# Cross attention on one core: P times values in runs of one to three tiles, maximum products chunk by chunk, and other slots for keys, values and the turning

## The reference

```
x = x + attention(layernorm(x))                 # token and channel diffusion
x = x + cross(layernorm(x), ctx_1024)           # the stage that the change touches
x = x + experts(layernorm(x))                   # top 2 of 8 experts

cross(query, value):                            # 16 heads, depth 8
    q, k, v = query @ wq.T + bq, value @ wk.T + bk, value @ wv.T + bv
    attn = softmax(q k^T / sqrt(8))             # per head, 56 x 1500
    return (attn v) @ wo.T + bo
```

## Time and profile before

| | |
|---|---|
| median of 3 runs | 646.7 us (645.82 to 649.69) |
| profiled execution | 653.12 us |
| its span, first to last instruction | 651.3 us |
| mean granted clock of TensorE | 0.96 |
| busy, share of the span | TensorE 91%, VectorE 66%, ScalarE 52%, GpSimd 28% |

### The profile page before, as it was taken

One profiled execution on the slowest core, in us unless ns is written; L12 is line 12 of the kernel. 1 busy time (PEld: TensorE's weight loads), 2 busy tenths in 40 slices (PEclk: granted clock), 3 DMA queues, 4 the chain that ended last, 5 costly groups with the idle time before them and its releaser, 6 DMA issues. The chain is left out here.

```text
span 651.3 us, 17561 instructions
## 1 busy us (share of the span) xinstructions
PE 593.1 (91%) x6732; PEld 481.7 (74%) x6732; DVE 427.2 (66%) x799; ACT 338.2 (52%) x506; POOL 183.2 (28%) x149
## 2 busy tenths in 40 slices
PE   3799787798999999999999999999985699999997
PEld 1566374376877877877877787787774589999997
DVE  4765357866887788778788788877822464444443
ACT  2466445274666576567566566657564353333321
POOL 4685305622223323224223232322100221111100
PEclk9789789798999999999999999999998599999999
DMA  5000006498267356446536736734620011111100
GB/s 211 1 3 3 0 3 133 94 193 192 68 132 183 96 140 144 119 117 142 144 92 141 172 88 127 179 100 91 144 100 1 17 46 49 48 48 48 48 17 29
DMA packets 26190, 60.29 MB, mean 93 GB/s; under 512 B 14368, under 2 KB 15392, under 8 KB 26152
## 3 DMA queue, kind: packets, MB, share of 16 engines
q1 hardware_dynamic: 26152, 59.77, 38.3%
HBM read 20.48 MB, written 0.46 MB: 32 GB/s over the span
## 5 line engine op out<-in xcount | busy, mean ns | idle before, releaser
L1163 DVE TENSOR_REDUCE chunk_max<-PS 128x1 f32<-128x500 f32 x336 | 214.3, 673 | 62.2 <-PE PS L1283 60.5
L1103 ACT ACTIVATE P<-PS 125x896 f32<-125x896 f32 x192 | 173.3, 913 | 124.1 <-PE PS L1307 123.4
L1283 PE MATMUL PS<-k_hi,q_block_hi 128*128 128x500 f32 x336 | 131.3, 438 | 6.5 <-ACT k_full L246 3.3
L1307 PE MATMUL PS<-q_stack,k_stack 97*125 97x224 f32 x768 | 122.5, 283 | 4.3 <-DMA q_stack<-neg_rows 2.4
L1307 PEld LDWEIGHTS PS<-q_stack,k_stack 97*125 97x125 f32 x768 | 106.9, 190 | 19.3 <-issue 8.9
L255 POOL TENSOR_TENSOR k_lo<-k_full,k_hi 128x500 fp32r<-128x500 f32 x48 | 61.1, 1276 | 104.7 <-ACT k_full L246 102.4
L1283 PEld LDWEIGHTS PS<-k_hi,q_block_hi 128*128 128x128 f32 x336 | 60.9, 193 | 37.1 <-ACT k_full L246 16.7
L1629 DVE TENSOR_TENSOR hidden<-gated,PS 128x448 f32<-128x448 f32 x64 | 39.6, 619 | 69.2 <-PE PS L1686 63.8
L1323 PE MATMUL PS<-P,values 125*32 125x112 f32 x3072 | 84.4, 262 | 0.6 <-ACT P L1103 0.5
L1323 PEld LDWEIGHTS PS<-P,values 125*32 125x32 f32 x3072 | 72.6, 110 | 14.3 <-issue 10.8
L1541 ACT ACTIVATE gated<-PS 128x448 f32<-128x448 f32 x64 | 34.8, 544 | 80.5 <-PE PS L1686 76.0
(11 more groups left out here) (153 smaller groups left out, 666.7 us busy)
## 6 DMA issues: line engine op xcount, KB each, us to landing
k_stack<-k_hi SPq DMA_DIRECT2D x128, 187.5 KB, 4.5
ctxT<-ctx_in SPq DMA_DIRECT2D x16, 750.0 KB, 4.3
k_stack<-k_lo SPq DMA_DIRECT2D x64, 187.5 KB, 4.4
w_gate_up<-wgu_in SPq DMA_DIRECT2D x8, 512.0 KB, 3.7
w_down<-wd_in SPq DMA_DIRECT2D x8, 256.0 KB, 2.7
q_stack<-neg_rows SPq DMA_DIRECT2D x112, 0.5 KB
mats<-mats_in SPq DMA_DIRECT2D x1, 832.0 KB, 5.2
q_copies<-q_hi SPq DMA_DIRECT2D x8, 98.0 KB, 4.4
```

Of the source, the lines that this page charges most:

```text
L1103: nc.scalar.activation(P[:, t % RING, :].rearrange("p (a n) -> p a n", a=2), PS[0:KR, 2 * (t % 2):2 * (t % 2) + 2, 0:HALF], ACT.Exp).then_ ...
L1163: nc.vector.tensor_reduce(out=chunk_max[:, n // KC, n % KC:n % KC + 1], in_=PS[:, max_bank(b, n), 0:KW], axis=AX.X, op=ALU.max).then_inc(m ...
L1283: nc.tensor.matmul(PS[:, max_bank(b, n), 0:KW], q_block_hi[:, j, 128 * t:128 * t + 128], k_hi[:, j, KW * c:KW * c + KW], start=True, stop= ...
L1307: last = nc.tensor.matmul(PS[0:KR, 2 * (t % 2) + g // 2, o:o + GH * N], k_stack[:, j, g, KR * t:KR * t + KR], q_stack[0:SHIFT_ROW + 1, j, ...
```

## The change

The runs of P times values get places of their own: `PLACES` has for each slot five numbers, maximum products, tiles of P times values, maximum products, tiles, maximum products. Twelve tiles a period are spread over slots 0 (two and two), 4 (one and one), 6 (two), and 8 to 11 (one each). Four tiles are still carried into slot 0 of the next period. The key and value products both come in slots 1, 3 and 8 (before, 2, 3, 4 and 1, 6, 7), the turnings in 4 and 8 (before, 3 and 8), the copy of the sums in 0 (before 1), denominators in 1 (before 2), both inversions in slot 1 (before 3 and 4), and the scaling in 3 (before 4). Of the 21 maximum products the first twelve are still those of query tiles 0 to 3, but ordered by chunk of keys, and the last nine those of tiles 4 to 6, by chunk too. Seven of them, before eight, belong to slots 8 to 11. On SP's queue the shift rows of the second half come ahead of the wait for the values and the load of the context.

```
-            MAX_PLACES = [(2, 0, 2), (0, 0, 0), (1, 2, 0), (1, 0, 0), (0, 1, 0), (1, 0, 1),
-                          (1, 0, 0), (1, 0, 0), (1, 0, 0), (2, 1, 1), (0, 0, 1), (0, 1, 1)]
-            KEY_SLOTS, VALUE_SLOTS, TURN_SLOTS = [2, 3, 4], [1, 6, 7], [3, 8]
-            SUMS_SLOT, DEN_SLOT, INVERT_SLOTS, SCALE_SLOT, OUT_SLOT = 1, 2, [3, 4], 4, 8
-            RING, QUAD, WEIGH_SLOTS = 6, 4, [0, 5, 9]
+            EARLY, CARRIED = 8, 4
+            PLACES = [(2, 2, 2, 2, 1), (1, 0, 0, 0, 0), (1, 0, 0, 0, 0), (0, 0, 0, 0, 0), (0, 1, 0, 1, 1), (0, 0, 1, 0, 0), (2, 2, 1, 0, 0), (1, 0, 1, 0, 0), (0, 0, 0, 1, 1), (0, 0, 2, 1, 0), (1, 1, 2, 0, 0), (0, 0, 0, 1, 1)]
+            KEY_SLOTS, VALUE_SLOTS, TURN_SLOTS = [1, 3, 8], [1, 3, 8], [4, 8]
+            SUMS_SLOT, DEN_SLOT, INVERT_SLOTS, SCALE_SLOT, OUT_SLOT = 0, 1, [1, 1], 3, 8
+            RING = 6
+            MAX_PLACES = [(first, second, third) for first, _, second, _, third in PLACES]
+            WEIGHED = [sum(n + m for _, n, _, m, _ in PLACES[:t]) for t in range(KT)]
+            TILE_ORDER = [0, 1, 2, 3, 4, 5, 6]
+            HALF_TILES = [slice(0, 4), slice(4, QT7)]
+            MAX_ORDER = ([(place, c) for c in range(KC) for place in range(0, 4)]
+                         + [(place, c) for c in range(KC) for place in range(4, QT7)])
...
                         if exists(b + 1, B):
                             load_stack(b + 1, 1 - j)
                             load_shift(b + 1, 1 - j, 0)
+                            load_shift(b + 1, 1 - j, 1)
                         if exists(b + 3, B):
                             sp.wait_ge(v_projected, KC * (b + 2))
                             load_ctx(sp, b + 3, 1 - j)
-                        if exists(b + 1, B):
-                            load_shift(b + 1, 1 - j, 1)
...
+                    def weigh_tiles(b, j, first, count):
+
+                        for i in range(first, first + count):
+                            if i >= CARRIED:
+                                weigh(b, j, i - CARRIED)
+                            elif later(b, 1):
+                                weigh(b - 1, 1 - j, KT - CARRIED + i)
...
                             if exists(mb, B):
                                 for n in first:
                                     max_scores(mb, mj, n)
+                            weigh_tiles(b, j, WEIGHED[t], PLACES[t][1])
...
-                            if t in WEIGH_SLOTS:
-                                q = WEIGH_SLOTS.index(t) - 1
-                                for w in range(QUAD):
-                                    if q >= 0:
-                                        weigh(b, j, QUAD * q + w)
-                                    elif later(b, 1):
-                                        weigh(b - 1, 1 - j, KT - QUAD + w)
+                            weigh_tiles(b, j, WEIGHED[t] + PLACES[t][1], PLACES[t][3])
```

More of the change, by code:

```diff
@@ L842, in build @@
         with s2:
-            EARLY = 8
-            MAX_PLACES = [(2, 0, 2), (0, 0, 0), (1, 2, 0), (1, 0, 0), (0, 1, 0), (1, 0, 1),
-                          (1, 0, 0), (1, 0, 0), (1, 0, 0), (2, 1, 1), (0, 0, 1), (0, 1, 1)]
-            KEY_SLOTS, VALUE_SLOTS, TURN_SLOTS = [2, 3, 4], [1, 6, 7], [3, 8]
-            SUMS_SLOT, DEN_SLOT, INVERT_SLOTS, SCALE_SLOT, OUT_SLOT = 1, 2, [3, 4], 4, 8
-            RING, QUAD, WEIGH_SLOTS = 6, 4, [0, 5, 9]
-            HALF_TILES = [slice(0, -(-HALF // 128)), slice(-(-HALF // 128), QT7)]
+            EARLY, CARRIED = 8, 4
[7 more added lines that the diff above has]
+            HALF_TILES = [slice(0, 4), slice(4, QT7)]
             HALF_ROWS = HALF_TILES[0].stop
+            MAX_ORDER = ([(place, c) for c in range(KC) for place in range(0, 4)]
+                         + [(place, c) for c in range(KC) for place in range(4, QT7)])
+            FIRST_OF_CHUNK = {MAX_ORDER.index((0, c)): c for c in range(KC)}
+            NEEDS_SECOND_HALF = min(n for n in range(QT7 * KC) if TILE_ORDER[MAX_ORDER[n][0]] >= 3)
             TURNING_BANKS = [4, 5, 7]
@@ L977, in load_shift @@
                         sp.wait_ge(rows_ready, 2 * b + a + 1)
-                        for r, t in enumerate(range(HALF_TILES[a].start, HALF_TILES[a].stop)):
+                        for r, t in enumerate(TILE_ORDER[HALF_TILES[a]]):
                             sp.dma_start(q_stack[SHIFT_ROW:SHIFT_ROW + 1, j, 128 * t:128 * t + 128].bitcast(F32),
@@ L1162, in take_max @@
                         dve.wait_ge(max_scored, QT7 * KC * b + n + 1)
-                        nc.vector.tensor_reduce(out=chunk_max[:, n // KC, n % KC:n % KC + 1],
+                        nc.vector.tensor_reduce(out=chunk_max[:, MAX_ORDER[n][0], MAX_ORDER[n][1]:MAX_ORDER[n][1] + 1],
                                                 in_=PS[:, max_bank(b, n), 0:KW], axis=AX.X, op=ALU.max
@@ L1210, in period @@
                             if later(b, 1):
-                                if t in INVERT_SLOTS:
-                                    invert(b - 1, INVERT_SLOTS.index(t))
+                                for a in range(2):
+                                    if INVERT_SLOTS[a] == t:
+                                        invert(b - 1, a)
                                 if t == SCALE_SLOT:
@@ L1272, in max_scores @@
                                 pe.wait_ge(first_blocks, 1)
-                        if n < KC:
-                            pe.wait_ge(k_hi_ready, KC * b + n + 1)
+                        if n in FIRST_OF_CHUNK:
+                            pe.wait_ge(k_hi_ready, KC * b + FIRST_OF_CHUNK[n] + 1)
                         if later(b, 1):
@@ L1277, in max_scores @@
                         else:
-                            if n == 3 * KC:
+                            if n == NEEDS_SECOND_HALF:
                                 pe.wait_ge(first_blocks, 2)
@@ L1281, in max_scores @@
                                 pe.wait_ge(max_taken, n - 3)
-                        t, c = n // KC, n % KC
+                        place, c = MAX_ORDER[n]
+                        t = TILE_ORDER[place]
                         nc.tensor.matmul(PS[:, max_bank(b, n), 0:KW], q_block_hi[:, j, 128 * t:128 * t + 128],
@@ L1399, in _ @@
                     pipelined(pe, period, B)
-                    for w in range(QUAD):
-                        weigh(B - 1, 1, KT - QUAD + w)
+                    for t in range(KT - CARRIED, KT):
+                        weigh(B - 1, 1, t)
                     denominators(B - 1)
```

## The result

The changed kernel takes 660.28 us (median of 4 runs, 659.29 to 661.21) against 646.35 us for the kernel before (4 runs): 13.9 us more, ratio 1.0189, 95% interval 1.0141 to 1.0237. The forecast was 656.5 us in a range of 647 to 664, so it is 3.8 us low and inside. The profiled execution of the changed kernel took 659.81 us, with a span of 658.0 us at a mean granted clock of 0.97.

What follows compares the result with a forecast made beforehand. TensorE was taken to bound the cross-attention. Twelve full periods +13.8 us, second −.4, first −2.0, last but one 0, last −1.6: +9.8 on 646.7 gave 656.5 us, range 647 to 664.

Steps and rivals of the forecast that it cites:

- The period: Each full cross-attention period: six more P times values runs less the waits removed, taken as +1.15 us.
- the .09 for the exponentials at tile 0: At a period's end, the scores' wait for exponentials (.53 for .44 us) would go, saving .09 us.
- six runs more: Nine P times values runs a period instead of three, each costing .34 us whatever its length: +2.04 us a period.
- waits removed: TensorE's waits in a period, .70 us on key banks and .09 on exponentials, would go: −.79 us together.
- the forecast's check: Check of the new order for new waits, VectorE keeping up in slot 0 included: taken as zero, .3 for the range.
- The first period: Shift rows sent ahead of the ctx load would give back 2.0 us of TensorE's wait (range 0 to 2.2).
- .5 us of room: In slot 8 the turning stands behind value and output products, 1.8 us against ScalarE's 1.34, so it would fit.
- The second period: No .50 clock after the shift-row wait, saving 1.5 us, while the longer period costs 1.1: −.4 us.
- The end: Last period but one 0, both effects meeting; last −1.6 us, two four-tile runs fewer starving ScalarE, less pairs and singles.
- (b): Rival, 20%: no measurable change; P times values runs cost .2 us, not .34, giving 647 us.
- (c): Rival, 8%: faster; only a drain is paid, .1 us a run, giving 639 us.
- (d): Rival, 15%: slower still; key waits merely moved, +.3 to +.79 us a period more, giving 660 to 666 us.

## Why the prediction was right, point by point

**The period.** Forecast +1.15 us, measured 24.59 − 23.45 = +1.14. Both terms held in the place they were put: nine runs of .33, and no wait for key banks left. Of the .09 for the exponentials at tile 0 about half went: the scores there take .44 and .52 us in turn (319.44 to 319.88, 294.86 to 295.38). Over the twelve full periods it is 281.69 us before and 294.95 after, +13.3 where +13.8 was forecast; half of the missing .5 is in the last of them, 23.64 before and 24.51 after.

**What that number hid.** The sum treated "six runs more" and "waits removed" as two independent terms, and the trials show that they are not. In the new slots three runs cost as much as nine (24.6 and 24.59), five .8 less. The price of a run is real, .31 where only one is added; but in this layout the short runs also pay for themselves in waits on VectorE, which the forecast's check had only looked for with the nine runs in place. The waits that longer runs would bring are held off by the spread. That the slots alone would free the key banks was argued and turned out right for the most part: with eight runs in the old slots the waits stay, with three runs in the new ones 3.6 of 14.0 us are left in the window (182 to 460 us in each), at the product behind the turning of slot 4, and with a run in that slot none. The waits on VectorE I had not seen.

**The first period.** Forecast −2.0, measured 23.98 against 23.90, +.1. This step failed. The sum gave the first period no runs to pay for, though it has seven of them where it had two. The wait for the last shift row did go, to .17 us, and the trial that puts the queue order back brings 1.0 us of it and 1.2 us of period. But I had set the gain against a period otherwise bound by the transfers, and TensorE's own work had grown beside them. Five runs more in it are 1.7 us. The granted clock is .50 in its first 2 us (scores take .81 us to the next start), where it was 1.00 in the profiled execution of before (.43); that is a difference of the two executions, as .50 stands there with the old slots too, in the trial of the queue order. And the turning of slot 8 waits for the bank of the third key, where my check had given .5 us of room:
```profile
138.57 1.01 PE L217 MATMUL PS<-ctxT,mats 128*128 128x500 f32 x2
139.41 1.04 PE L225 MATMUL PS<-mats,ctxT 128*125 128x128 f32 x8
141.07 0.30 PE L1300 MATMUL PS<-consts,max_turn 128*128 128x128 f32 x1 [0.61 <-ACT k_full L246]
```
That room was made of the output product, which the first period does not have. In the later full periods it holds. What was to be won was also smaller than the 2.21 us: this wait was read off one execution, which took 653.12 us where no timed one beside it took more than 649.69, and in the six other traces with the old order it is at most 1.42.

**The second period.** Forecast −.4, measured 24.59 − 24.92 = −.3: the clock no longer falls behind the wait. It is right against that one execution of before; no other trace with the old order shows the fall of the clock, so in the median there was hardly a 1.5 to win.

**The end.** Forecast 0 and −1.6; measured 21.01 against 20.45, +.6, and 13.8 against 15.1 from the last tile 0 to the last scores, −1.3. The last period's saving is near the 1.6 worked out. ScalarE's gaps are .23 at single tiles in place of the 1.38 at a run of four, here in ScalarE's timeline of the last period but one:
```profile
485.13 0.92 ACT L1108 ACTIVATE P<-PS 125x896 f32<-125x896 f32 x1 [0.88 <-PE PS L1314]
486.28 0.92 ACT L1108 ACTIVATE P<-PS 125x896 f32<-125x896 f32 x1 [0.23 <-PE PS L1314]
```
In that period, however, single runs also make TensorE the slower of the two: 1.15 us from start to start, the 1.16 of the working.

**The sum.** +13.3 − .3 + .1 + .6 − 1.3 = +12.4 us in the stage against +9.8 forecast, and 13.9 between the medians. The 2.6 us are the first period (2.1) and the last but one (.6), less the rest. The last 1.5 us lie within the spread of the runs of before (645.82 to 649.69), whose median here is the lowest of five sets; in the others it was 648.1 to 649.3. So the number was right by its largest term, the twelve periods, whose mechanism the trials bear out, and not by luck; the 3.5 us for the start pulled it low, and the change of the queue order, timed alone, doesn't show them. Of the rivals, (b) and (c) are refuted as prices: a run costs .31 to .33 and not .2 or .1. The measured time touches the 660 that (d) had, but by other terms: (d) did not come in steady periods, though its mechanism of waits that are only moved is what the trials with three and five runs ran into.

## What to carry to other kernels

Where a run of small products costs the same whatever its length, count runs and not products, and read the price off three distances of starts: ahead of it, within it, behind it. Then ask what the run covers. Between products whose reader is slower than TensorE a run is time for the reader, so the number of runs and their places can't be chosen apart: three long runs at the ends of bursts cost as much as nine short ones, and three in the middle of bursts beat both. A margin found for the steady period must be checked again for the first one, where some of the work that makes it is missing.

## What the runs showed of the hardware

With 12 moving columns, a product of rounded f32 operands puts nothing on the product ahead and .08 us on the one behind, with 32 and with 128 columns of weights alike. One of plain f32 operands puts .09 ahead and .10 behind with 32 columns, and nothing ahead and about .09 behind with 128. The Trainium skill (TensorEngine Tiling (Array Packing), Key Properties) has the drain at a change of mode, and among the restrictions that column tiling excludes the transpose mode of f32 and rounded f32 input, which no run here tests. These runs don't show whether the rounded products are laid in the same mode as their neighbours or not.
